# Dissolving a block of parameter preparation into the projection block ahead of it

## What is computed

```python
    x = x + _L0_attn_ref(_layernorm(x), ...)   # per-channel linear state space, then x @ Wout
    x = x + _L0_ffn_ref(_layernorm(x), ...)    # 64 experts, top 8 by sigmoid, plus a shared expert
    x = x + _L1_attn_ref(_layernorm(x), ...)   # attention on cos/sin features, V = x @ W_v.T + b_v, out @ W_out.T
    x = x + _L1_ffn_ref(_layernorm(x), ...)    # 8 experts, top 2, relu squared
    x = x + _L2_attn_ref(_layernorm(x), ...)   # linear attention with elu, a 3-tap convolution, then Wp
    x = x + _L2_ffn_ref(_layernorm(x), ...)
    x = x + _L3_attn_ref(_layernorm(x), ...)   # k, v, r from x mixed with the token before; a scan; Wo
    x = x + _L3_ffn_ref(_layernorm(x), ...)
```

## Time and profile before

| what | us |
|---|---|
| median of 3 runs | 1958.83 (1954.51 to 1964.04) |
| time of the profiled execution | 1963.8 |
| its span | 1961.8 |
| TensorE busy | 1723.9 (88%) |
| VectorE busy | 1198.0 (61%) |
| ScalarE busy | 974.3 (50%) |
| GpSimd busy | 847.5 (43%) |

### The profile page before, as it was taken

One profiled execution on the slowest core, in us unless ns is written; L12 is line 12 of the kernel. 1 busy time (PEld: TensorE's weight loads), 2 busy tenths in 40 slices (PEclk: granted clock), 3 DMA queues, 4 the chain that ended last, 5 costly groups with the idle time before them and its releaser, 6 DMA issues.

```text
span 1961.8 us, 25458 instructions
## 1 busy us (share of the span) xinstructions
PE 1723.9 (88%) x8004; PEld 1314.2 (67%) x8004; DVE 1198.0 (61%) x2815; ACT 974.3 (50%) x1864; POOL 847.5 (43%) x852
## 2 busy tenths in 40 slices
PE   6989998659999998989999988888899888888799
PEld 6979997537767676767777655666665555555565
DVE  5552215658677767777776835544446666677765
ACT  3612002346556665665656567676545444445442
POOL 3842101225545454554555454443447666651100
PEclk9989558769999999999999989898999888889999
DMA  5001000168433333233324462231000101112233
GB/s 84 1 2 24 1 1 1 38 146 201 111 92 102 87 98 92 90 99 86 96 90 118 114 161 73 58 88 47 17 23 23 33 23 26 23 28 75 81 106 94
DMA packets 131182, 134.92 MB, mean 69 GB/s; under 512 B 56614, under 2 KB 75306, under 8 KB 131050
## 3 DMA queue, kind: packets, MB, share of 16 engines
q1 hardware_dynamic: 120904, 132.35, 25.3%
q10 hardware_dynamic: 10146, 0.94, 0.6%
HBM read 127.93 MB, written 5.31 MB: 68 GB/s over the span
## 4 chain that ended last, share of the span: by engine, by line
PE 36%; DVE 17%; ACT 11%; issue 7%; POOL 4%; DMA 2%; SPq 1%; DVEq 0%; ACTq 0%; POOLq 0%
PE ypsum L1122 7%; PE flow_G L100 4%; PE flow_G L102 3%; PE flow_G L101 3%; DVE flow_a L1666 2%; DVE flow_a L1672 2%; DVE flow_phi L1450 2%; DMA flow_raw<-in_L_ffn_expert_down_k 2%; POOL flow_alo L1753 2%; PE flow_U L100 2%; PE flow_U L101 2%; PE flow_U L102 1%; ACT flow_ahi L1152 1%; ACT xn_tokens L1184 1%; PE flow_side L100 1%
## 5 line engine op out<-in xcount | busy, mean ns | idle before, releaser
L1753 POOL TENSOR_TENSOR flow_alo<-flow_a,flow_ahi 128x512 fp32r<-128x512 f32 x264 | 342.0, 1295 | 345.6 <-ACT flow_ahi L1152 345.1
L100 PE MATMUL flow_G<-xn_hi,flow_hi 128*128 128x512 f32 x520 | 285.6, 549 | 49.5 <-DVE flow_a L1666 23.2
L1666 DVE TENSOR_TENSOR flow_a<-flow_G,flow_mask 128x512 f32<-128x512 f32 x256 | 175.7, 686 | 161.2 <-ACT flow_G L1326 137.9
L1326 ACT ACTIVATE flow_G<-flow_G 128x512 f32<-128x512 f32 x256 | 149.0, 582 | 140.2 <-PE flow_G L102 139.7
L101 PE MATMUL flow_G<-xn_lo,flow_hi 128*128 128x512 f32 x520 | 213.0, 410 | 0.0
L102 PE MATMUL flow_G<-xn_hi,flow_lo 128*128 128x512 f32 x520 | 211.7, 407 | 0.0
L1672 DVE TENSOR_TENSOR flow_a<-flow_U,flow_a 128x512 f32<-128x512 f32 x296 | 204.7, 691 | 9.9
L1152 ACT ACTIVATE flow_ahi<-flow_a 128x512 fp32r<-128x512 f32 x264 | 165.4, 627 | 85.3 <-DVE flow_a L1672 84.1
L1762 POOL TENSOR_TENSOR flow_b<-flow_b,flow_mask 128x512 f32<-128x512 f32 x96 | 127.1, 1329 | 147.3 <-ACT flow_b L1330 76.7
L100 PEld LDWEIGHTS flow_G<-xn_hi,flow_hi 128*128 128x128 f32 x520 | 102.7, 197 | 117.6 <-issue 44.6
L1762 POOL TENSOR_TENSOR flow_a<-flow_a,flow_mask 128x512 f32<-128x512 f32 x96 | 127.8, 1343 | 106.3 <-ACT flow_a L1330 54.7
(11 more groups left out here) (536 smaller groups left out, 3930.1 us busy)
## 6 DMA issues: line engine op xcount, KB each, us to landing
flow_mask<-mask_rows_top SPq DMA_DIRECT2D x512, 128.0 KB, 3.1
flow_mask<-mask_rows_top SPq DMA_DIRECT2D x64, 256.0 KB, 3.3
flow_mask<-mask_rows_zone SPq DMA_DIRECT2D x64, 256.0 KB, 3.2
flow_mask<-mask_rows_steps SPq DMA_DIRECT2D x32, 256.0 KB, 4.0
x<-in_L_attn_x SPq DMA_DIRECT2D x8, 256.0 KB, 5.5
flow_raw<-in_L_ffn_expert_gate_k SPq DMA_DIRECT2D x16, 128.0 KB, 3.6
flow_raw<-in_L_ffn_expert_up_k SPq DMA_DIRECT2D x16, 128.0 KB, 3.6
flow_raw<-in_L_ffn_expert_down_k SPq DMA_DIRECT2D x16, 128.0 KB, 4.1
```

The costliest lines, as they stand in the source:

```text
L100: pe.matmul(out, w_hi, x_hi, start=start, stop=False)
L1326: act.activation(gate, gate, ACT.Silu).then_inc(ev["r_done"], 1)
L1666: dve.tensor_tensor(out, G[at % 2].psum[:, :], weight, ALU.mult).then_inc(ev["t_done"], 1)
L1753: pool.tensor_tensor(alo[i][:, :], acts[i][:, :], ahi[i][:, :].bitcast(F32), ALU.subtract)\
```

## The change

The prepare block goes. A class `Prepare` keeps its steps as methods, and the projection calls them between its own steps. The parameter loads are issued at the start of the projection by ScalarE (14) and SyncE (14), and SyncE then issues the first two loads of expert weights (6 DMAs), into their final place. The moving of transposed matrices, the taps, the products and the high parts go from VectorE to ScalarE, behind its steps 2, 4 and 6; the exponents go behind step 8, and there are two table loads in them instead of three. TensorE's transposes go behind its steps 1 and 3 and its products behind step 5, through two PSUM banks instead of five. GpSimd makes the index tables ahead of its first group and the 14 low parts behind its last. VectorE keeps two fills, two small operations behind step 0, which wait for all small loads, and five small ones behind step 9. The results are written to DRAM behind the last mask rows, and nobody waits for either at the end of the block; instead ScalarE, VectorE and GpSimd wait for them (`rows_gone`) at the start of the flow. The tiles of layer 1's parameters are allocated before the scan.

```diff
@@ class Moe
+    def first_loads(self, sp):
+        for load in range(self.slots):
+            self.load_one(sp, load)
+
+    def load(self, sp, lo_split, after):
+        for load in range(self.load_of(self.all - 1) + 1):
             if load >= self.slots:
                 sp.wait_ge(lo_split, (load - self.slots + 1) * self.step)
-            here = slot * self.step
-            for i, src in enumerate(self.sources):
-                experts, chunks = src.shape[1], self.chunks
-                out = self.raw[:, i, here:here + self.step, :]
-                if at < chunks:
-                    src = src[:, at * experts // chunks:(at + self.step) * experts // chunks, :]
-                else:
-                    src = self.shared[i]
-                    out = self.raw[0:64, i, here, :] if i == 2 else self.raw[:, i, here, 0:64]
-                sp.dma_start(out, src).then_inc(self.loaded[slot], 16)
-            if after is not None:
-                after(load)
+                self.load_one(sp, load)
+            after(load)
+
+    def load_one(self, sp, load):
+        at, slot = load * self.step, load % self.slots
+        here = slot * self.step
...
@@ in place of load_attn
+class Prepare:
...
+        self.bank = [k.ps(f"prep{i}", stack=stack) for i in range(2)]
...
+    def load_some(self, eng, half):
+        k = self.k
+        with k.nc.allow_non_contiguous_dma(reason="a few columns of parameters"):
+            for t, src in self.loads[:self.squares][half::2]:
+                eng.dma_start(t, src).then_inc(k.params_in, 16)
+            for t, src in self.loads[self.squares:][half::2]:
+                eng.dma_start(t, src).then_inc(self.ev["in"], 16)
+
+    def keep(self, sp):
+        k = self.k
+        sp.wait_ge(self.ev["kept"], 2)
+        for l in (2, 3):
+            sp.dma_start(k.later_rows[l], self.later[l][:, :].bitcast(F32)).then_inc(k.later_out, 16)
+
+
+    def turn_squares(self, pe):
+        k, ev = self.k, self.ev
+        pe.wait_ge(k.params_in, self.first_total)
+        for i in range(8):
+            last = pe.transpose(self.part(i), self.raw[self.turns[i][0]][:, :], k.ident[:, :])
+            if i % 4 == 3:
                 last.then_inc(ev["turned"], 1)
+
+    def turn_others(self, pe):
+        k, ev, bank, raw = self.k, self.ev, self.bank, self.raw
+        pe.wait_ge(ev["in"], self.total)
+        pe.wait_ge(ev["copied"], 4)
+        pe.transpose(bank[0][:, 0:128], raw["L3_attn_Wr"][:, :], k.ident[:, :])
+        pe.transpose(bank[0][:, 128:192], raw["shell"][:, :], k.ident[0:64, 0:64])
+        pe.transpose(bank[0][0:64, 192:224], raw["omega"][:, :], k.ident[0:32, 0:32]).then_inc(ev["turned"], 1)
+        pe.wait_ge(ev["copied"], 8)
+        for m in range(5):
+            last = pe.transpose(bank[1][0:64, m * 64:(m + 1) * 64], raw["combine"][:, m * 64:(m + 1) * 64],
+                                k.ident[0:64, 0:64])
+        last.then_inc(ev["turned"], 1)
+
+    def multiply(self, pe):
+        k, ev, raw = self.k, self.ev, self.raw
+        pe.wait_ge(ev["taken"], 1)
+        out = self.bank[0]
+        pe.matmul(out[:, 0:128], raw["L1_attn_W_v"][:, :], self.wout_t[:, :], start=True, stop=True)
+        pe.matmul(out[:, 128:129], self.wout_t[:, :], raw["b_v"][:, :], start=True, stop=True)
+        pe.matmul(out[:, 129:130], k.a["wp_t"], raw["conv_b"][:, :], start=True, stop=True).then_inc(ev["pe2"], 1)
+
+
+    def take_squares(self, act):
+        ev, raw, a = self.ev, self.raw, self.k.a
+        act.wait_ge(ev["in"], self.total)
+        for m in "kvr":
+            act.activation(self.rest[m][:, :], raw[f"mix_{m}"][:, :], ACT.Identity, scale=-1.0, bias=1.0).then_inc(ev["rest"], 1)
+        for i in range(8):
+            if i % 4 == 0:
+                act.wait_ge(ev["turned"], i // 4 + 1)
+            self.take(act, i)
+
+    def take(self, act, i):
+        ev, raw, a = self.ev, self.raw, self.k.a
+        name, out = self.turns[i]
+        if out is not None:
+            act.activation(out, self.part(i), ACT.Copy).then_inc(ev["copied"], 1)
+        else:
+            m = name[-1].lower()
+            act.activation(a[f"now_{m}"][0][:, :], self.part(i), ACT.Copy, scale=raw[f"mix_{m}"][:, 0:1])
+            act.wait_ge(ev["rest"], 3)
+            act.activation(a[f"old_{m}"][0][:, :], self.part(i), ACT.Copy, scale=self.rest[m][:, 0:1]).then_inc(ev["copied"], 1)
+
+    def take_others(self, act):
+        ev, raw, a, bank = self.ev, self.raw, self.k.a, self.bank
+        act.wait_ge(ev["turned"], 3)
+        self.take(act, 8)
+        act.activation(a["shell_w"][0][:, 0:64], bank[0][:, 128:192], ACT.Copy)
+        act.activation(a["shell_w"][0][:, 64:65], raw["charge"][:, :], ACT.Copy)
+        act.wait_ge(ev["small"], 1)
+        act.activation(a["omega_t"][0:64, 0:32], bank[0][0:64, 192:224], ACT.Copy).then_inc(ev["taken"], 1)
+        act.wait_ge(ev["turned"], 4)
+        for m in range(5):
+            act.activation(a["combine_t"][:, m * 64:(m + 1) * 64], bank[1][0:64, m * 64:(m + 1) * 64], ACT.Copy, scale=self.mags[m])
+        act.wait_ge(ev["copied"], 9)
+        for j in range(3):
+            last = act.activation(a[f"tap{j}"][0][:, :], a["wp_t"], ACT.Copy, scale=raw["conv_w"][:, j:j + 1])
+        last.then_inc(ev["whole"], 1)
+
+    def take_products(self, act):
+        ev, raw, a, out = self.ev, self.raw, self.k.a, self.bank[0]
+        act.wait_ge(ev["pe2"], 1)
+        act.activation(a["vo_bias"][:, :], out[:, 128:129], ACT.Identity, bias=raw["b_out"][:, 0:1])
+        act.activation(a["wp_bias"], out[:, 129:130], ACT.Identity, bias=raw["bp"][:, 0:1])
+        act.activation(a["vo_w"][0][:, :], out[:, 0:128], ACT.Copy).then_inc(ev["whole"], 1)
+        act.wait_ge(ev["whole"], 2)
+        for full, hi, _ in self.pairs:
+            act.activation(hi, full[:, :], ACT.Copy).then_inc(ev["hi"], 1)
+
+    def exponents(self, act):
+        ev, raw, a = self.ev, self.raw, self.k.a
+        act.activation(self.e0[:, :], raw["log_temp"][:, :], ACT.Abs).then_inc(ev["act"], 1)
+        act.wait_ge(ev["act"], 1)
+        act.activation(self.e1[:, :], self.e0[:, :], ACT.Exp, scale=-1.0).then_inc(ev["act"], 1)
+        act.wait_ge(ev["tables"], 3)
+        act.activation(self.distant[:, :], self.dist[:, :], ACT.Exp, scale=-0.3 / 10.0)
+        act.activation(a["w_log"], raw["decay"][:, :], ACT.Exp).then_inc(ev["act"], 1)
+        act.wait_ge(ev["act"], 2)
+        act.activation(self.e2[:, :], self.e1[:, :], ACT.Ln, bias=1.0).then_inc(ev["act"], 1)
+
+    def fill(self, dve):
+        ev, raw, a = self.ev, self.raw, self.k.a
+        dve.memset(a["omega_t"][:, :], 0.0).then_inc(ev["temp"], 1)
+        dve.wait_ge(ev["temp"], 1)
+        dve.memset(a["omega_t"][64:65, 32:33], 1.0).then_inc(ev["small"], 1)
+        dve.wait_ge(ev["in"], self.total)
+        dve.tensor_scalar(a["rff"][:, 0:32], raw["rff_row"][:, :], 1.5707963267948966, None, ALU.add)
+        dve.tensor_copy(a["rff"][:, 32:64], raw["rff_row"][:, :])
+
+    def temperature(self, dve):
+        ev, raw, a = self.ev, self.raw, self.k.a
+        link = Chain(dve, ev["temp"], 1)
+        dve.wait_ge(ev["act"], 4)
+        link.then(dve.tensor_scalar(self.e0[:, :], raw["log_temp"][:, :], 0.0, 0.1, ALU.max, ALU.add))
+        link.then(dve.tensor_tensor(self.e0[:, :], self.e0[:, :], self.e2[:, :], ALU.add))
+        link.then(dve.reciprocal(self.inv_temp[:, :], self.e0[:, :]))
+        dve.tensor_scalar(a["decay"][:, :], self.distant[:, :], self.inv_temp[:, 0:1], None, ALU.mult)
+        dve.tensor_scalar(a["w_log"], a["w_log"], -1.0, None, ALU.mult).then_inc(ev["kept"], 1)
+
+    def tables(self, pool):
+        a, dist = self.k.a, self.dist
...
+    def low(self, pool):
+        ev = self.ev
+        for i, (full, hi, lo) in enumerate(self.pairs):
+            pool.wait_ge(ev["hi"], i + 1)
+            last = pool.tensor_tensor(lo, full[:, :], hi.bitcast(F32), ALU.subtract)
+        last.then_inc(ev["kept"], 1)
@@ send_masks
 def send_masks(k, sp, r):
@@ -545,8 +575,6 @@
         sp.wait_ge(k.masks_done, r.index * GROUPS + g + 1)
         sp.dma_start(rows[:, g * GROUP:(g + 1) * GROUP], k.weights_t[0:r.e, g * GROUP:(g + 1) * GROUP])\
           .then_inc(k.mask_out[g], 16)
-    for g in range(GROUPS):
-        sp.wait_ge(k.mask_out[g], 16 * (r.index + 1))
@@ flow; called first by ScalarE, VectorE and GpSimd
+        def rows_gone(eng):
+            for g in range(GROUPS):
+                eng.wait_ge(k.mask_out[g], 16)
+            eng.wait_ge(k.later_out, 32)
@@ project
+        prep = Prepare(k, st)
...
+        k.ffn0 = ffn0(k.io)
+        k.ffn0.count_loads(k)
+        k.ffn0.raw = k.at("flow_raw", [P, 3, 4, P], F32, k.raw_at)
+        assert k.spot() <= k.raw_at
...
-        def turns(body):
+        k.ffn0 = ffn0(k.io)
+        k.ffn0.count_loads(k)
+        k.ffn0.raw = k.at("flow_raw", [P, 3, 4, P], F32, k.raw_at)
+        assert k.spot() <= k.raw_at
+
+        def turns(body, eng, **between):
```

(20 more changed lines are left out.)

264 lines of the change are left out of this document (85 added, 179 removed).

## The result

The changed kernel takes **1941.58 us** (median of 5 runs, 1939.14 to 1946.45) against 1958.83 for the one before, beside each other 0.9911 of its time, with an interval of 0.9889 to 0.9933. The forecast was 1939.5, the range 1931 to 1951. (Five runs of the kernel before, taken beside these, have the same median as the three quoted above.) The profiled execution took 1942.1 us, its span is 1940.4.

The account below looks back on a forecast made before the run. A nearly idle 36.1 us hole between projection and flow lay on the path, then a DMA-leaning flow start. 29.5 off the hole, less 11.5 projection growth, plus 1.3 in the flow: 19.3 us saved, 1939.5 us, range 1931 to 1951.

Parts of the forecast that it names:

- The hole: Between last routing eviction and first expert split: 36.1 us shrinks to 6.6, mostly the write of kept constants; 29.5 us go.
- The front: Start of the projection: VectorE's wait for small parameters makes the residual add of group 3 come 4.5 us late.
- The middle: ScalarE's first two pieces of added work exceed its gaps in the projection by 1.7 us each; 0.5 us comes through.
- the clock: Falls of TensorE's granted clock in waits behind ScalarE's new stops add 2 us to the projection, between 0 and 8.
- Products and high parts: ScalarE's third piece, 5.0 us ahead of the last group's normalisation with a 1.9 us gap, adds 3.1 us.
- The exponents: End of the projection: ScalarE's exponents, 3.9 us with two table loads, delay the last eviction by 1.4 us.
- GpSimd: Its nine table instructions and 14 subtractions, 11 us at most, cost nothing or some tenths and are ready for the write.
- Rival (b): Replacement wait is longer: late parameters, slower wide activations, or GpSimd subtractions taking 22 us; saving 12 to 13, 1946; chance 0.17.
- The flow: Start of the flow: with both first expert loads already in, the second split does not wait; 1.3 us gained.
- rival (d): Early expert loads save nothing because the write of the constants ends last anyway; costs 1.3 us, 1941; no chance given.
- (a): ScalarE's stops keep TensorE at 1.2 GHz through the projection; saving 0, 1958 us; chance 0.07.
- (c): TensorE enters the flow cold and stays so, each 10 us costing up to 10 more; kernel slower; chance 0.04.

Follow-up runs that it names:

- the second pair: The kernel before and the changed kernel each profiled once more without an edit, both starting the projection at TensorE's low clock; 1967.4 and 1942.39 us.
- the third: Changed kernel with exponents behind ScalarE's step 0, temperature behind VectorE's step 4 and the write ahead of the last two mask rows; 1936.01 us.
- the seventh: Changed kernel with all three edits: phases behind VectorE's step 2, exponents behind ScalarE's step 0, write ahead of the last two mask rows; 1934.13 us.
- the last run: Changed kernel with phases, exponents and write all moved earlier, plus filler transposes in TensorE's waits; 1931.92 us, 0.9852 of the kernel before.

## Why the prediction was right

By its steps:

- **The hole.** Forecast 36.1 to 6.6, measured 8.1. That the write bounds it is shown: moved ahead by two mask rows it leaves 2.9. Its size was off by 1.5 us, because the write took longer here than in the place from which its duration was taken: its second half landed after 6.8 us instead of 5.5. The flow's mask loads are 0.3 of it, the mask rows ahead of it are not the cause, as said above; the rest stays open. One of the prediction's signs, no hole of over 8 us, was missed by 0.1.
- **The front, 4.5 us.** Measured 3.5 in the pair of profiles in which TensorE starts at 2.4 GHz (and falls sooner in the changed kernel), 0.9 in the pair that starts at 1.2. The wait was foreseen well: until 335.76, forecast 334.8 for a stage that starts 0.9 earlier, and the add behind it 335.94 against 335.3. What the step lacked is the other path to the same add, TensorE's two slow output projections and the logits, which is as long when the clock is low. With the wait taken away the front at the low clock was no shorter, and from a start like the change's it was 1.1 us shorter. So most of the 3.5 is not shown to be the wait's: TensorE was also slower in that front than in the one it is compared with, and how much that made is open. That the measured term came near 4.5 is in part luck.
- **The middle, 0.5, and the clock, 2.** Start to the add of group 7 grew by 6.3 us, 3.5 of it front; so 2.8 for these two together, forecast 2.5. By the second pair it is 3.8 in all (45.4 to 49.2), 2.9 of them behind the front. In the first pair 1.6 of the 2.8 are waits of VectorE for an output projection that ran at the low clock (0.44 and 1.21 us): that is the clock's. Another 0.9 are its waits for ScalarE's high part, which can't be told apart. The two pieces themselves were overrated: 3.6 us each were forecast, 2.2 each it took (348.56 to 350.77 and 360.74 to 362.90), for the reason that stands under the next point.
- **Products and high parts, 3.1 us.** Measured 2.2 (4.0 to 6.2). This term was mis-sized, first, by one choice: I took 0.3 us for an activation from the duration in its row. The 14 high parts of the change have durations of 0.29 but start 0.20 apart (374.97, 375.17, 375.37), and those that read PSUM 0.16 apart; with a scale per row it is 0.25 from PSUM and 0.29 from SBUF (the three taps, 362.03 to 362.90). The 17 took 3.4 us (374.00 to 377.37), not 5.0. Second, the gap into which they fall was 1.1 us and not 1.9. Without them group 7 would have been normalised 4.0 us behind its add, as before, at 375.6. ScalarE came to them only at 374.00, because it had idled 2.66 us for TensorE's logits ahead of the affinity of 373.02, and an eviction of 0.5 us follows them. 3.4 less 1.1 is 2.3, and 2.2 was measured. Here the Trainium skill (ScalarE: Activation LUTs, "What ACT_TABLE_LOAD costs") bears on it: it gives an activation of N columns 186 ns and 0.833 ns per column, with 93 ns more for each operand read per partition, and says that successive ones overlap by about 93 ns. For 128 columns that makes, as an estimate from that page, 0.29, and 0.20 between starts, or 0.29 with a scale per row. The rows of the high parts and of the taps agree; those that read PSUM are 0.04 closer together, with a scale or without.
- **The exponents, 1.4 us.** Measured 1.2, by the profile of the change and by the run that moved them. The tables are loaded in 1.28 us each (385.46 to 386.75, 387.48 to 388.77), and the next activation starts 0.01 us after the load ends. The rule of the Trainium skill (ScalarE: Activation LUTs, "What ACT_TABLE_LOAD costs") that gives a switch a further drain of about 1.38 us is not borne out in either place.
- **GpSimd, nothing.** Its 14 subtractions ran from 375.52 to 381.59, 0.41 us apart, half the 0.80 of the earlier trace rows, and ended 10 us before the write. Rival (b) had its strongest leg there.
- **The flow, 1.3 us.** Measured 2.7 in one pair and 0.6 in the other (92.75 to 92.2); the kernel before alone differs by 3.6 between its two profiles (96.4 and 92.75), so these pairs do not resolve a term of 1.3. Without the early loads the hole got longer by 2.5 us and the flow's part stayed 92.4: what they save lies in the hole, since a load issued behind the write lands after it. The forecast let the write cover both loads; rival (d), that they save nothing, is wrong by the profile, though no median shows it: without the early loads it was 1939.91, not slower.
- **Rivals (a) and (c).** From 400 to 420 us the clock was 0.85, from 450 to 460 it was 1.00; the projection grew by 6 to 10 us, not by 30.

The sum of the steps was 19.3 us, the profiled pair gives 20.15 at the flow's first normalisation, the medians of the result 17.3. Misses of opposite sign made the sum good, which is luck: the hole lost 1.5 us less than forecast and the stage began 0.8 later, the projection grew 1.8 less and the flow gained 1.4 more.

## What to carry to other kernels

When a serial block is dissolved into a stage, the gain is the hole less the last wait that remains in it, and that wait should get its own place in the order: issuing the slow write ahead of two mask rows took 5 us off the hole, the most that any single edit took off a stretch of the profile, and 2 to 4 of them reached the flow. For a train of small instructions count the distance of their starts, not their durations. And before a few microseconds in one stage are explained by an edit, profile the same kernel twice, and compare executions in which the stage began at a like clock: that alone made 6 us here in a kernel without any edit.

## What the hardware showed that was not expected

- The projection of the kernel before took 55.65 and 61.6 us in two executions, the difference being TensorE's granted clock, 0.89 against 0.61 from 324 to 340 us. All of it lies ahead of the last normalisation; the 12.2 us behind that are equal to 0.02.
- Filler work of 8 transposes in each of TensorE's waits (32 in the first) kept the clock at 1.00 from 348 to 372 us in both kernels that have it. In the median the changed kernel gained little by it (1941.58 to 1938.37, the intervals overlap), as did the variant with all three edits (1934.13 to 1931.92, where they overlap too).
- A write of 1.73 MB from SBUF to DRAM landed 5.5 us after the issue of its second half in one place and 6.8 in another, though both moved data at some 400 GB/s. The flow's mask loads are not the reason: with them held back it was 6.5. Nor is the mask row issued just ahead of it: in the third, the seventh and the last run one is, and it was 5.5 to 5.7. The cause was not found.
